# Moving the first batch's attention rows between the last expert tiles, and the last output tile ahead of a statistics step

## The reference

```python
x = x + 0.5 * ffn(layernorm(x))            # top-1 of 8 experts: 128 -> 512 -> relu -> 128
y = layernorm(x)
y = y + linear_attention(layernorm(y)*g1+b1)   # 16 heads of 8, phi = elu+1
y = y + lookup_gelu((layernorm(y)*g2+b2) @ w1) @ w2
x = x + y
x = x + 0.5 * ffn(layernorm(x))            # the same experts again
```

## Time and profile before

| what | value |
|---|---|
| median of three runs | 214.22 us (213.69 to 214.76) |
| the profiled execution | 215.13 us, of which 213.4 us are the span from the first to the last instruction |
| PE busy | 190.5 us (89%) |
| DVE, ACT, POOL busy | 124.7, 107.5, 119.8 us |
| mean granted clock of PE | 0.968 of full speed |
| first expert pass, PE | from 30.2 to 78.4 us of the span |
| attention of the first two batches | about 78.7 to 94 us |

### The profile page before, as it was taken

The page is one execution under the profiler, slowest core; times in us unless marked ns, Lnnn a source line. Parts: engine busy times, 40 slices in busy tenths (PEclk is TensorE's granted clock), DMA queues, the critical chain, the costliest instruction groups (busy, mean ns, idle before and its releaser), DMA issues.

```text
span 213.4 us, 4550 instructions
## 1 busy us (share of the span) xinstructions
PE 190.5 (89%) x1414; PEld 159.3 (75%) x1414; DVE 124.7 (58%) x528; ACT 107.5 (50%) x316; POOL 119.8 (56%) x186
## 2 busy tenths in 40 slices
PE   5997839999999888888989999989698999899992
PEld 2763339999999876677775769679335999899991
DVE  4688811222222773988797674777433776677762
ACT  2630004665556479747878863510301666466670
POOL 7872277755586445743777531857770245355544
PEclk9998875999999999999999999999969999999999
DMA  5999688779996231299990000011119838586700
GB/s 160 228 388 342 170 286 318 226 249 327 264 285 187 59 80 37 77 418 416 415 420 20 2 3 0 27 40 43 40 54 324 305 103 283 182 278 203 258 25 0
DMA packets 29752, 40.26 MB, mean 189 GB/s; under 512 B 4229, under 2 KB 20392, under 8 KB 28704
## 3 DMA queue, kind: packets, MB, share of 16 engines
q1 hardware_dynamic: 23968, 33.58, 44.3%
q0 software_dynamic: 2496, 4.76, 8.7%
q10 hardware_dynamic: 3264, 1.62, 2.6%
HBM read 10.78 MB, written 14.46 MB: 118 GB/s over the span
## 4 chain that ended last, share of the span: by engine, by line
PE 54%; POOL 13%; DMA 11%; DVE 9%; issue 8%; ACT 2%; SPq 1%; POOLq 0%; DVEq 0%
PE bank L985 14%; PE bank L1000 13%; PE bank L1122 6%; PE bank L842 5%; PE bank L1138 5%; POOL xnT L570 5%; DMA xnT<-slot_scratch,posu 3%; DMA eqrq<-row_scratch 2%; PE bank L978 2%; POOL h L579 2%; DMA Xg<-xn_scratch,srcu 2%; DMA out_dram<-ysb,eqrq 2%; DMA rb<-in_L_ffn_router_b_dram 2%; POOL ew L627 1%; PE bank L889 1%
## 5 line engine op out<-in xcount | busy, mean ns | idle before, releaser
L681 ACT ACTIVATE hT<-bank,ewc_own 128x128 f32<-128x128 f32 x184 | 52.6, 369 | 63.8 <-PE bank L985 62.9
L985 PE MATMUL bank<-xT,ewc_own 128*128 128x128 f32 x368 | 50.8, 283 | 0.6 <-DVE xT L1349 0.6
L1000 PE MATMUL bank<-ew,hT 128*128 x368 | 49.6, 279 | 0.0
L985 PEld LDWEIGHTS bank<-xT,ewc_own 128*128 128x128 f32 x368 | 46.6, 198 | 1.5 <-issue 1.0
L1000 PEld LDWEIGHTS bank<-ew,hT 128*128 128x128 f32 x368 | 45.6, 195 | 0.4 <-issue 0.4
L617 POOL DMA_INDIRECT out_dram<-ysb,eqrq x23 | 22.5, 979 | 29.5 <-DVE ysb L1359 26.2
L549 POOL DMA_INDIRECT Xg<-xn_scratch,srcu x23 | 22.0, 957 | 15.3 <-PE bank L978 7.5
L842 PE MATMUL bank<-ones_bf 128*128 128x512 bf16 x83 | 25.8, 446 | 3.4 <-POOL ident L466 2.6
L1355 DVE TENSOR_TENSOR ysb<-bank,ewc_own 128x128 f32<-128x128 f32 x23 | 6.7, 290 | 28.9 <-PE bank L1000 28.8
L609 POOL DMA_INDIRECT row_scratch<-pay,posu x16 | 15.8, 987 | 10.9 <-DVE posu L1317 7.6
L570 POOL DMA_INDIRECT xnT<-slot_scratch,posu x16 | 15.4, 962 | 10.5 <-DMA slot_scratch<-ysb 6.7
(11 more groups left out here) (226 smaller groups left out, 296.8 us busy)
## 6 DMA issues: line engine op xcount, KB each, us to landing
ewc_own<-ew SPq DMA_DIRECT2D x46, 322.0 KB, 4.0
row_scratch<-xn SPq DMA_DIRECT2D x8, 1024.0 KB, 10.6
ew<-in_L_ffn_W_dram SPq DMA_DIRECT2D x1, 2048.0 KB, 11.8
ew<-in_L_ffn_W_dram SPq DMA_DIRECT2D x8, 256.0 KB, 7.7
slot_scratch<-ysb SPq DMA_DIRECT2D x23, 64.0 KB, 2.6
eqrq<-row_scratch SPq DMA_DIRECT2D x15, 70.0 KB, 2.3
x<-in_L_attn_x_dram SPq DMA_DIRECT2D x4, 256.0 KB, 3.8
xn_scratch<-xn ACTq DMA_DIRECT2D x4, 256.0 KB, 6.9
```

What stands on the lines that cost most here:

```text
L681: last = A(hT[:, t.slot, c * P:(c + 1) * P], up_bank(k, c)[:, c * P:(c + 1) * P], ACT.Relu, scale=0.5 if m else 1.0, bias=ewc[t.ahead][:, ...
L985: last = mm(up_bank(k, c)[:, c * P:(c + 1) * P], ewc[t.ahead][:, c * P:(c + 1) * P], xT[:, t.slot, :], start=True, stop=True)
L1000: last = mm(bank[4 + t.parity][:, 0:D], hT[:, t.slot, c * P:(c + 1) * P], ew[:, bass.ds(e[k], 1), W2_AT + c * D:W2_AT + (c + 1) * D].squee ...
```

## The change

In the first expert pass the following moves. The guess for batch 0 (`guess_rstd(0)` on ACT) goes from behind tile 20's relu to behind tile 19's, and its refinement (`finish_rstd(0)` on DVE) from step 20 to step 19, which is in front of `take_x(22)`. ACT makes the rows of batch 0 in two halves, blocks 0 and 1 behind tile 20's relu and blocks 2 and 3 behind tile 21's, instead of all four behind tile 22's. PE turns them in front of the last `down` (`turn_first`, the same four transposes) instead of after it and the warm-up. On ACT, `norm1(0)` then stands ahead of `guess_rstd(1)`. On PE, only the values of batch 0 (bank 4) wait for the last `take_y`, no longer the keys. On DVE, the second half of batch 1's `take_back`, with the variances, goes from step 21 to step 22, so from before to behind the last `take_y`. No instruction of work is added or removed.

```diff
--- before.py
+++ after.py
@@ -24,7 +24,7 @@
 NV = NG * NE
 TPE = TOK // P
 UPTO = [(S * (g + 1) + NE * (P - 1)) // P for g in range(NG)]
-BACK = {17: (0, 1), 18: (2, 3), 20: (4, 5), 21: (6, 7)}
+BACK = {17: (0, 1), 18: (2, 3), 20: (4, 5), 22: (6, 7)}
 
 
 PARTS = 2
@@ -683,8 +683,21 @@
                     last.then_inc(hT_ready, 1)
                     if m == 1:
                         chances(k)
+                    elif k == 19:
+                        guess_rstd(0)
                     elif k == 20:
-                        guess_rstd(0)
+                        normal1(0, range(2))
+                    elif k == 21:
+                        normal1(0, range(2, GT))
+
+            def normal1(b, part=range(GT)):
+
+                act.wait_ge(a_ready, b + 1)
+                for j in part:
+                    t = b * GT + j
+                    last = A(h1[:, b % 2, j, :], x[:, t, :], ACT.Identity, scale=rstd[:, t, 1:2], bias=shift[:, t, 1:2])
+                if part[-1] == GT - 1:
+                    last.then_inc(h1_ready, 1)
 
             def guess_rstd(b):
 
@@ -726,13 +739,6 @@
                 A(h1T[:, b % 2, :], bank[0][:, :], ACT.Identity, scale=gb[:, 0:1], bias=gb[:, 1:2]
                   ).then_inc(h1T_ready, 1)
 
-            def normal1(b):
-
-                act.wait_ge(a_ready, b + 1)
-                for t in range(b * GT, (b + 1) * GT):
-                    last = A(h1[:, b % 2, t % GT, :], x[:, t, :], ACT.Identity, scale=rstd[:, t, 1:2], bias=shift[:, t, 1:2])
-                last.then_inc(h1_ready, 1)
-
             def attention_input(b):
 
                 act.wait_ge(a_ready, b + 1)
@@ -780,9 +786,8 @@
                 act.wait_ge(attT_ps, b + 1)
                 A(attT[:, b % 2, :], bank[1][:, :], ACT.Copy).then_inc(attT_ready, 1)
 
-            normal1(0)
+            norm1(0)
             guess_rstd(1)
-            norm1(0)
             normal1(1)
             take_kv(0)
             take_q(0)
@@ -968,6 +973,13 @@
                     last = mm(bank[4][:, 0:NT], inr[:, t, :], inq[:, t, :], start=t == 0, stop=t == T - 1)
                 last.then_inc(src_ps, 1)
 
+            def turn_first():
+
+                pe.wait_ge(h1_ready, 1)
+                for j in range(GT):
+                    last = nc.tensor.transpose(bank[0][:, j * P:(j + 1) * P], h1[:, 0, j, :], ident[:, :])
+                last.then_inc(h1T_ps, 1)
+
             def experts(m, e):
                 def turn(k):
                     t = Tile(k)
@@ -1014,6 +1026,8 @@
                         turn(k + 2)
                     if k + 1 < NT:
                         up(k + 1)
+                    if m == 0 and k + 1 == NT:
+                        turn_first()
                     down(k)
 
             turn_xn(0, 0)
@@ -1054,11 +1068,11 @@
 
             def keys_values(b):
                 pe.wait_ge(h1T_ready, b + 1)
-                if b == 0:
-                    pe.wait_ge(y_ready, NT)
                 if b >= 1:
                     pe.wait_ge(v_out, b)
                 for bk, at, done in ((3, 0, k_ps), (4, D, v_ps)):
+                    if b == 0 and bk == 4:
+                        pe.wait_ge(y_ready, NT)
                     for j in range(GT):
                         last = mm(bank[bk][:, j * D:(j + 1) * D], h1T[:, b % 2, j * P:(j + 1) * P],
                                   wkv[:, at:at + D], start=True, stop=True)
@@ -1140,7 +1154,6 @@
                     if j + 1 == GT or b + 1 == B:
                         last.then_inc(w2_ps, 1)
 
-            turn1(0)
             for b in range(B):
                 keys_values(b)
                 queries(b)
@@ -1397,7 +1410,7 @@
                     if m == 1:
                         rest_of_rows(k)
                     take_y(k)
-                    if m == 0 and k == 20:
+                    if m == 0 and k == 19:
                         finish_rstd(0)
                     if m == 0 and k in BACK:
                         take_back(BACK[k])
```

## The result

The changed kernel takes 217.88 us (median of four runs, 216.85 to 219.64) against 213.95 us for the kernel before in the same measurement. The ratio is 1.0206, 95% interval 1.016 to 1.0252: **slower by about 4.4 us**, where 2.1 us were forecast. The profiled execution took 216.85 us, of which 215.1 are the span.

A forecast was written before the change was run, and what follows sets the result against it. It took batch 1's second take_back half as heading the chain that sets the end; 1.00 us from order plus 1.14 from ACT's lateness, 2.14 on the 214.22 us median, gave 216.4 us, range 213.4 to 217.6.

The forecast's parts named there:

- What bounds the kernel: After the first expert pass, the second half of batch 1's take_back heads the chain; POOL has 1.7 us to spare.
- ScalarE's lateness and the last down: Relus of tiles 20 and 22 come 1.00 and 1.14 us late; PE's last down ends at 79.55 instead of 78.41.
- The last output tile: DVE's last take_y starts at 79.58 instead of 79.35, 0.23 us later, which alone costs nothing.
- take_back behind it: On DVE, take_back starts 2.14 us late: 1.00 from the order alone, 1.14 from ACT's lateness.
- What the early turn gives: Batch 0's keys go out at about 79.8 instead of 80.65; nothing gained, as take_kv(0) stands behind normal1(1).
- The clock: PE runs at full clock, 1.00; a longer hole until 84.46 could halve it, but the forecast priced no fall.
- Rival 4: PE's clock falls to half: 24 products in the chain cost 2.5 us more, 218.8 us; chance 0.05.
- hand over without slack: From normal1(1) to finish_rstd(2), ACT, PE and DVE have no slack, so all 2.14 us reach POOL's rows of batch 2.
- The sign: Whole kernel: slower with chance 0.72, same (213.15 to 215.29 us) 0.16, faster 0.12.
- Rival 1: Batch 0 leads: PE's keys come sooner, 1.31 us gained, 212.9 us; chance 0.12.
- rival 3: POOL's gathers decide, through when tile 22 is taken, or later slack absorbs the loss: 213.3 to 214.4 us; chance 0.08.
- Rival 2: ACT keeps pace if batch 0's variances come early; only DVE's new order counts: +1.0, 215.2 us; chance 0.16.

The follow-up runs named there:

- experiment 3: The kernel before with only the second half of batch 1's take_back moved to step 22, behind the last output tile: 215.85 us, ratio 1.0073.
- experiment 18: The kernel of 12 with finish_rstd(1) in step 21 ahead of the last take_y and guess_rstd(1) ahead of norm1(0): 212.8 us, ratio 0.9955.
- experiment 2: The changed kernel with the second half of batch 1's take_back put back in step 21, ahead of the last output tile: 214.73 us, ratio 1.0038.
- experiment 10: The changed kernel with take_back in step 21, take_kv(0) ahead of normal1(1) on ScalarE, sum_kv(0) ahead of turn1(1) on TensorE: ratio 1.0033.
- experiment 1: The changed kernel with nine warm-up products on TensorE between batch 0's queries and the turn of batch 1: 216.3 us, ratio 1.0093.
- 11: The changed kernel with both halves of batch 1's take_back earlier, in steps 19 and 20: ratio 1.0035.
- 5: The kernel of experiment 1 with POOL's scaling of the expert biases moved behind POOL's rows of batch 2: ratio 1.0187, in a disturbed group.
- 6: The kernel before with only POOL's scaling of the expert biases moved behind POOL's rows of batch 2: ratio 1.0007, in a disturbed group.
- 12: The kernel of 11 with POOL's scaling also moved behind its rows of batch 2: ratio 1.0015.
- experiment 14: The kernel of 5 run again, unaltered: ratio 1.0187, in a disturbed group.

## Why the prediction was wrong

**What bounds the kernel: right.** `take_back` of blocks 6 and 7 is the head of the chain. Later (experiment 3, changed kernel) costs what it is late; sooner, with guess and refinement freed (experiment 18), gains: 17.43 us to POOL's rows of batch 2 against 18.54.

**ScalarE's lateness and the last down: right to 0.1 us.** Forecast were 1.00 and 1.14 us for the relus of tiles 20 and 22; the last is 4.09 us behind the variances instead of 3.01, so 1.08. The last output tile, 0.23 us later by forecast, came 0.20 later. The four transposes were hidden.

**take_back behind it: right.** 2.14 us forecast, 2.13 measured; experiment 3 gives the order alone 1.02 (forecast 1.00). ScalarE's lateness counts little without the new order (0.35, experiment 2) and in full with it, as the working had it.

**What the early turn gives: right that it gives nothing, wrong that it costs nothing.** The keys went out early (77.76 us, 6.83 behind the variances instead of 7.70) and `take_kv(0)` did not follow. But they are then missing behind the wait: in experiment 3 they follow an idle time of 2.33 us and the clock stays, in the changed kernel they lie in front of one of 2.00 us and it falls.

**The clock: this step failed.** I had the hole in the text, "from 79.8 on, and then nothing until 84.46", and took the clock as 1.00 with 0.95 of the chance, because the kernel before kept it through a wait of 1.31 us. In the run the granted clock was 0.50 from 85 to 91 us, and that added 2.25 us which the sum had at nothing. That row could not bear the conclusion: it is one shorter wait, with the keys behind it and not in front. The Trainium skill, "TensorE: Matmul & The Clock Gate", section on the HAM clock gate, says that the slow clock is the default and that activity lifts it; the prediction cited this and hardly weighed it. The trace agrees: the clock fell behind 2.00 and 1.03 us of idleness with 0.66 us of products between them. But a longer hole alone does not predict it either (experiment 3: 2.33 us, clock 1.00; experiment 2: 0.21 us, clock 0.50), so what exactly decides stays open.

Rival 4's price, 2.46 us for 24 products, is close to the measured 12.98 - 10.73 = 2.25, in part by luck: TensorE's part cost about 2.8 us, and 0.6 of that were hidden by a slack of ScalarE's guess that the prediction did not see ("hand over without slack"). So rival 4's 218.8 us is close to the measured 217.88 and 218.35. Forecast and clock term together, 2.13 + 2.25 = 4.38 us, agree with the 4.4 us (3.4 to 5.4) of the times.

**The sign and the other rivals.** Slower was right. Rival 1 (batch 0 leads) is refuted by the changed kernel, where the early keys wait for `take_kv(0)`, and by experiment 10, rival 3 (POOL) by 3, where the tile came sooner and the time rose. Rival 2 gives the right price for the order alone, but its condition did not come true.

## What to carry to other kernels

Work moved forward leaves a gap where it was. If a tensor engine with little to do loses the work that stood behind its wait, the clock can fall, and the products behind the gap then take nearly twice as long (eight of them 2.09 us instead of 1.16). One profile of the kernel before does not tell whether it will, and the length of the hole does not either, so give that case a price and a real chance instead of nothing. Ask of each step in an in-order list what stands in front of it, on every engine that it passes through: here the guess on ScalarE and the refinement on VectorE were each held up by another tile's work, the two waits ended within 0.1 us of each other, and the two moves together brought the rows 1.07 us forward.

## What the runs showed of the hardware

A VectorE instruction that starts about 0.1 us after POOL's 128x1056 `tensor_scalar` is held up by about 0.8 us: 1.16 instead of 0.34 us for a `scalar_tensor_tensor` (experiments 1 and 3), 0.94 or 0.95 instead of 0.17 for the first `avar` step (experiments 2, 10 and 11). It follows POOL's instruction when that is moved (5, 6, 12 and 18: one instruction of `combine(3)` takes 1.15 us instead of 0.34). The kernel before escapes by its timing: its scaling starts 0.13 us before a `batch_norm_stats`, which is not held up. In the changed kernel `combine(2)` starts 1.0 us after the scaling and runs beside it at its usual 1.13 us. The Trainium skill, "SBUF — State Buffer", section on the two separate sides, describes a port pair that VectorE and POOL share and that one of them holds for its whole instruction while the other is blocked. A shared resource fits; a block for the whole 2.9 us is not what the traces show.

Of the clock: with nine products in the gap it stayed up in experiment 1 and fell in experiment 14 all the same, behind expert tiles that had been waiting. It fell behind idle times of 0.21, 1.03 and 0.65 us (experiment 2) and stayed up behind one of 2.33 us (experiment 3). What a fall costs depends on what waits for TensorE: 2.25 us in the changed kernel, about 0.3 in experiment 2. How close the kernel before is to a fall, the runs do not tell.
